# Sum of squares of y taken along the rows of a transposed copy, a prologue that projects the first half of x before the second is normed, and the row order 7, 3, 6, 2, 5, 1, 4, 0

## Chip, core and metric

One core of one Trainium2 chip. The metric is the device time of one execution in microseconds (us). The three runs of the kernel before took 556.85, 557.12 and 557.29 us; their median is 557.12.

## What is computed

`xn` is the layer norm of x (1024 rows of 256). Sixteen heads of width 128 attend causally over it, and a small 256 x 256 product of `xn` is added; the sum with x is the output.

```python
q = (x @ Wq).reshape(B, T, H, D)
k = (x @ Wk).reshape(B, T, H, D)
v = (x @ Wv).reshape(B, T, H, D)
q = rmsnorm(q, q_rms_w)
k = rmsnorm(k, k_rms_w)
scores = jnp.einsum('bthd,bshd->bhts', q, k) * scale + bias[None]
scores = jnp.where(causal[None, None], scores, -jnp.inf)
attn = jax.nn.softmax(scores, axis=-1)
y = jnp.einsum('bhts,bshd->bhtd', attn, v)
y = rmsnorm(y, subln_w)
y = y.transpose(0, 2, 1, 3).reshape(B, T, H * D)
return y @ Wproj
```

`rmsnorm` divides a row by the root of the mean of its squares. This is the place of the change: for each head and each row of y the kernel needs the sum of 128 squares.

## The kernel before

The program is written out by hand, engine by engine, with semaphores. x is cut into 8 row tiles of 128 rows. Every fp32 product is made of three fp32r matmuls, high by high, high by low and low by high (`product`, L469 to L473), so each operand is stored as a high part (rounded by ScalarE) and a low part (the rest, by VectorE or GpSimd).

Each engine runs the same two-level loop: 16 heads, and in a head 8 steps s. `ORDER` (L33) says which row tile i a step works on; row tile i has i+1 blocks of 128 columns, because of the causal mask. A step on TensorE holds: the scores of the next step's row (`score`, L531), one or two of the eight projections of the next head (`project`, L504: six matmuls of 384 columns, q, k and v together), a part of the attention product (`attend`, L555), and at the end the transposes of this step's probabilities (`transpose_probs`, L544). The eight rows form two groups of four, `GROUPS`: the first four of `ORDER` and the last four. `attend` multiplies a group by v, in two halves, into the one bank `yT_ps`; y comes out transposed, 128 columns of D on the partitions and 4 x 128 rows along the free side. The second group of a head is attended to in steps 0 and 1 of the next head.

y is normed late. ScalarE squares `yT_ps` (`y_out`, L755) into `y_sq`; since D lies on the partitions there, the sum over D is a matmul: `sum_squares` (L576) multiplies four tiles of `y_sq` by a column of ones, which the trace shows as eight matmuls with one output column each. VectorE adds EPS times the squared row sum (`y_mean`, L907), GpSimd takes the power -0.5 (`norm_y`, L422), and VectorE scales the output product by it when it adds that to `acc` (`add_out`, L916). `sum_squares` of group 0 stands at step 0 of the next head, in the bank `qkv_ps`, that of group 1 at step 4, in `yT_ps`.

The engines' other work in a head: ScalarE copies each projection out (`copy_qkv`, L714), squares q and k, takes the exponentials (`exps`, L739) and the high parts. VectorE adds bias and takes the row maximum (`mask`, L874), makes the low parts (`probs_lo`, `qk_lo`, `y_lo`) and the sums of the q and k squares (`mean_squares`, L854). GpSimd splits weights and v and norms q and k (`norm_qk`, L382), whose result `transpose_qk` (L521) waits for. `score` of a next head's first row waits for the last `qk_lo`.

Prologue: x comes in two transfers. VectorE takes the moments of half 0, then of half 1, then norms half 0 (`normed`, L943), and later half 1. TensorE runs 24 warming matmuls, transposes all of x (`transpose_x`, L605) and only then projects the head 0. The fp8 weights are decoded by eight VectorE operations (L982 to L989) before the first `mean_squares`.

Of the kernel before, what the change touches and what calls it, by code (L numbers as in the profile page):

```python
# [13 lines left out]
def build_block(nc, x, wq, wk, wv, wproj, q_w, k_w, sub_w, ffn_w, ffn_ws, ffn_xs, out):  # L14
# [18 lines left out]
    ORDER = [7, 0, 6, 1, 5, 2, 4, 3]  # L33
# [16 lines left out]

    def misc_done(h, job):
# [5 lines left out]
        base = NPAIR + len(MISC_FIRST) + (h - 1) * len(MISC)  # L57
        if isinstance(h, int) and h == H - 1:
            return base + MISC_LAST.index(job) + 1
        if isinstance(h, int) and h == H:  # L60
            return base - len(MISC) + len(MISC_LAST) + MISC_TAIL.index(job) + 1
        return base + MISC.index(job) + 1
# [7 lines left out]
    with ctx:  # L70
# [11 lines left out]
        ones = sb("ones", [P, 1])  # L82
# [31 lines left out]
        y_sq = sb("y_sq", [P, 2, 4 * P])  # L114
# [23 lines left out]
        x_loaded = [sem(f"x_loaded{n}") for n in range(2)]  # L138
# [52 lines left out]
        ss_ready = sem("ss_ready")  # L191
# [34 lines left out]
        WARM_UP = 24  # L226

# [21 lines left out]
        def squares_of(h, k):  # L249

            if isinstance(h, int) and h == 0 and k % 2:
                return y_sq[:, 0, :].rearrange("p (t n) -> p t n", t=2)
# [32 lines left out]
        def _(sp):  # L285
            for n in range(2):
                half = slice(n * NT // 2, (n + 1) * NT // 2)
                sp.dma_start(acc[:, half, :], x_v[:, half, :]).then_inc(x_loaded[n], 16)
# [32 lines left out]
        def _(pool):  # L321
# [20 lines left out]
            pool.memset(ones[:, :], 1.0)  # L342
            for h in range(H):
                pool.memset(slopes[:, h:h + 1], float(np.float32(2.0 ** (-0.5 * (h + 1)))))

            for n in range(2):
# [4 lines left out]

            link(pool.iota(dist[:, :], pattern=[[-1, T]], base=T - P, channel_multiplier=1,
                           allow_small_or_imprecise_dtypes=True))
            pool.affine_select(out=dist[:, :], in_=dist[:, :], compare_op=ALU.is_ge, fill=BIG, base=T - P,
                               pattern=[[-1, T]], channel_multiplier=1).then_inc(const_ready, 1)
# [66 lines left out]
            def norm_y(h, g, now):  # L422

                pool.wait_ge(misc_read, misc_done(now, f"ss{g}"))
# [38 lines left out]
            norm_y(H - 1, 0, H)  # L463
            norm_y(H - 1, 1, H)
# [3 lines left out]
        def _(pe):  # L468
# [6 lines left out]
            def bank_free(h, job):  # L475
# [17 lines left out]
                if same:  # L493
# [10 lines left out]
            def project(h, par, k):  # L504
# [8 lines left out]
                if k == 1 and not (isinstance(h, int) and h <= 1):  # L513
                    pe.wait_ge(misc_read, misc_done(h - 1, "ss0"))
# [40 lines left out]
            def attend(h, par, g, half):  # L555
# [4 lines left out]
                if half == 0:  # L560
# [4 lines left out]
                    if g == 0 and not (isinstance(h, int) and h == 0):  # L565
                        pe.wait_ge(misc_read, misc_done(h, "ss1"))
# [32 lines left out]
            for _ in range(WARM_UP):  # L599
                pe.matmul(score_big[:, 0:4 * P], ident_b[:, :], ident_b[:, :].unsqueeze(1).broadcast_to([P, 4, P]),  # L600
                          start=True, stop=True)
# [11 lines left out]
            for n in range(2 * KT):  # L613
                transpose_x(n)
# [484 lines left out]
```

## Time and profile before

| | before |
|---|---|
| median of three runs | 557.12 us |
| the profiled execution | 556.8 us, of which the span of the trace 554.7 |
| granted TensorE clock, mean of the span | 0.991 |
| TensorE matmul busy | 531.1 us (96%) |
| TensorE weight loads busy | 492.5 us (89%) |
| VectorE busy | 414.6 us (75%) |
| ScalarE busy | 376.0 us (68%) |
| GpSimd busy | 333.8 us (60%) |
| the chain that ended last | TensorE 77%, GpSimd 9%, issue 4%, VectorE 3%, ScalarE 3% |

The chain of waits is followed back from the last instruction. Matmuls overlap one another: a matmul's duration in a row is from its start to its end in the array, while what it costs the stream is the distance to the start of the next one.

### The profile page before, as it was taken

To read this page: it belongs to the slowest core of one execution; us is meant where nothing else is said; L and a number is where in the kernel's file an instruction comes from. 1 tells how busy PE (TensorE), PEld (TensorE's weight loads), DVE (VectorE), ACT (ScalarE), POOL (GpSimd) and SP (SyncE) were. 2 spreads that over 40 slices of the span, in tenths; PEclk is the share of its full clock that TensorE was granted. 3 is DMA by queue.
4 is the path that set the end of the run, shared out by engine and by line. 5 is a ranking of instruction groups with operands and counts; after the bars stand their busy time and mean duration, and the time that the engine had idled before them with its cause. 6 is when DMAs were issued, how large, how long until landed. Compare 5 with 4: busy or idle time off the path is not lost.

```text
span 554.7 us, 12030 instructions
## 1 busy us (share of the span) xinstructions
PE 531.1 (96%) x3548; PEld 492.5 (89%) x3548; DVE 414.6 (75%) x999; ACT 376.0 (68%) x855; POOL 333.8 (60%) x431
## 2 busy tenths in 40 slices
PE   5768999999999999999999999999999999999996
PEld 2758899999989999998999999899999989999885
DVE  5867778686777868777786867778687786878765
ACT  2367778685776868577686857768685776858561
POOL 3386487683748658483776837486584847748121
PEclk9799999999999999999999999999999999999999
DMA  5100101001010100101010010101001000000002
GB/s 159 54 2 1 39 1 38 3 1 40 2 39 0 38 0 0 38 0 38 0 38 0 0 38 0 38 0 32 6 0 38 0 9 0 9 1 1 1 1 77
DMA packets 18582, 10.83 MB, mean 20 GB/s; under 512 B 2176, under 2 KB 18560, under 8 KB 18560
## 3 DMA queue, kind: packets, MB, share of 16 engines
q1 hardware_dynamic: 17568, 10.49, 6.3%
q8 instruction: 11, 0.18, 0.1%
q10 hardware_dynamic: 992, 0.07, 0.1%
q14 instruction: 11, 0.09, 0.1%
HBM read 9.51 MB, written 1.05 MB: 19 GB/s over the span
## 4 chain that ended last, share of the span: by engine, by line
PE 77%; POOL 9%; issue 4%; DVE 3%; ACT 3%; DMA 1%; POOLq 1%; DVEq 0%; SPq 0%
PE pT_ps L551 9%; PE qkv_ps L471 9%; PE qkv_ps L473 8%; PE qkv_ps L472 8%; PE yT_ps L473 6%; PE yT_ps L472 6%; PE yT_ps L471 6%; PE score_big L471 4%; PE score_big L473 4%; PE score_big L472 4%; PE misc L527 3%; POOL qk_n L220 3%; POOL qk_r L385 3%; PE qkv_ps L580 2%; PE yT_ps L580 2%
## 5 line engine op out<-in xcount | busy, mean ns | idle before, releaser
L723 ACT ACTIVATE stage<-qkv_ps 128x384 f32<-128x384 f32 x119 | 58.6, 493 | 91.1 <-PE qkv_ps L473 90.6
L897 DVE TENSOR_TENSOR pT_lo<-pT_ps,pT_hi 128x384 fp32r<-128x384 f32 (+1 forms) x192 | 100.9, 554 | 25.2 <-ACT pT_hi L751 23.3
L751 ACT ACTIVATE pT_hi<-pT_ps 128x384 fp32r<-128x384 f32 (+1 forms) x192 | 86.3, 484 | 46.7 <-PE pT_ps L551 42.9
L425 POOL TENSOR_TENSOR y_r<-y_ms,minus_half 128x4 f32<-128x4 f32 x32 | 32.8, 1026 | 136.1 <-DVE y_ms L913 136.1
L743 ACT ACTIVATE probs<-probs,neg_max 128x1024 f32<-128x1024 f32 (+7 forms) x128 | 98.4, 770 | 8.2 <-DVE neg_max L888 7.6
L551 PE MATMUL pT_ps<-ident,probs 128*128 128x128 f32 x576 | 85.7, 276 | 4.0 <-ACT probs L743 3.3
L471 PE MATMUL qkv_ps<-w_hi,xT_hi 128*128 128x384 f32 x242 | 87.3, 361 | 0.6 <-ACT stage L723 0.6
L473 PE MATMUL qkv_ps<-w_hi,xT_lo 128*128 128x384 f32 x242 | 81.9, 338 | 0.0
L472 PE MATMUL qkv_ps<-w_lo,xT_hi 128*128 128x384 f32 x242 | 81.8, 338 | 0.0
L385 POOL TENSOR_TENSOR qk_r<-qk_ms,minus_half 128x4 f32<-128x4 f32 x64 | 65.0, 1015 | 26.8 <-DVE qk_ms L862 26.0
L551 PEld LDWEIGHTS pT_ps<-ident,probs 128*128 128x128 f32 x576 | 66.8, 143 | 10.9 <-DVE pT_lo L897 4.2
L471 PE MATMUL yT_ps<-pT_hi,v_hi 128*128 128x256 f32 (+1 forms) x224 | 71.7, 320 | 0.4 <-DVE pT_lo L897 0.4
L473 PE MATMUL yT_ps<-pT_hi,v_lo 128*128 128x256 f32 (+1 forms) x224 | 71.9, 321 | 0.0
L472 PE MATMUL yT_ps<-pT_lo,v_hi 128*128 128x256 f32 (+1 forms) x224 | 71.7, 320 | 0.0
L859 DVE TENSOR_REDUCE qk_ms<-squares 128x4 f32<-128x512 f32 x62 | 42.5, 685 | 37.2 <-ACT squares L730 36.9
L888 DVE CUSTOM_DVE_ANT_0 probs<-score_big,bias 128x1024 f32<-128x1024 f32 (+1 forms) x64 | 65.0, 1016 | 1.9 <-PE score_big L473 1.9
L220 POOL TENSOR_TENSOR qk_n<-stage,qk_r 128x512 f32<-128x512 f32 x60 | 62.4, 1040 | 5.7 <-POOL qk_r L385 1.9
L402 POOL TENSOR_TENSOR v_lo<-stage,v_hi 128x256 fp32r<-128x256 f32 x62 | 46.6, 752 | 9.0
L471 PE MATMUL score_big<-kT_hi,qT_hi 128*128 128x512 f32 (+2 forms) x128 | 50.3, 393 | 1.8 <-DVE kT_lo L871 1.7
L471 PEld LDWEIGHTS qkv_ps<-w_hi,xT_hi 128*128 128x128 f32 x242 | 46.2, 191 | 2.1 <-ACT stage L723 0.9
L472 PEld LDWEIGHTS qkv_ps<-w_lo,xT_hi 128*128 128x128 f32 x242 | 45.9, 190 | 0.0
L473 PEld LDWEIGHTS qkv_ps<-w_hi,xT_lo 128*128 128x128 f32 x242 | 45.7, 189 | 0.0
(182 smaller groups left out, 1308.6 us busy)
## 6 DMA issues: line engine op xcount, KB each, us to landing
w_raw<-in_wq SPq DMA_DIRECT2D x16, 128.0 KB, 2.2
w_raw<-in_wk SPq DMA_DIRECT2D x16, 128.0 KB, 2.3
w_raw<-in_wv SPq DMA_DIRECT2D x16, 128.0 KB, 2.3
wp_raw<-in_wproj SPq DMA_DIRECT2D x16, 128.0 KB, 2.0
acc<-in_x SPq DMA_DIRECT2D x2, 512.0 KB, 5.5
out<-acc SPq DMA_DIRECT2D x8, 128.0 KB, 1.8
w<-in_ffn_w ACTq DMA_DIRECT2D x1, 64.0 KB, 6.2
q_col<-in_q_w ACTq DMA_DIRECT2D x1, 0.5 KB, 3.0
```

The lines of the kernel that those rows point to most:

```text
L220: eng.tensor_tensor(qk_n[:, k % 2], stage_of(h, k)[:, :, 0:2 * D].rearrange("p t (a d) -> p t a d", d=D), qk_r[:, k % 2, :].rearrange("p ( ...
L385: pool.tensor_tensor(qk_r[:, k % 2, :], qk_ms[:, k % 2, :], minus_half[:, 0:4], ALU.pow).then_inc(qk_r_ready, 1)
L402: pool.tensor_tensor(v_lo[:, par, 2 * k:2 * k + 2, :], v, v_hi[:, par, 2 * k:2 * k + 2, :].bitcast(f32), ALU.subtract).then_inc(v_split, 1)
L471: pe.matmul(dst, a_hi, b_hi, start=start, stop=False)
L472: pe.matmul(dst, a_hi, b_lo, start=False, stop=False)
L473: return pe.matmul(dst, a_lo, b_hi, start=False, stop=stop)
L551: last = pe.transpose(ps[:, (j - a) * P:(j - a + 1) * P], probs[:, s % 2, j * P:(j + 1) * P], ident[:, :])
L723: act.activation(stage_of(h, k // 2)[:, k % 2, :], qkv_bank(h, k)[:, 0:3 * D], ACT.Copy).then_inc(qkv_read, 1)
L743: act.activation(probs[:, s % 2, 0:(i + 1) * P], probs[:, s % 2, 0:(i + 1) * P], ACT.Exp, bias=neg_max[:, par, s:s + 1], scale=-1.0, accum ...
L751: act.activation(pT_hi[g][:, a:b, r * P:(r + 1) * P], pT_ps[(CHUNK0[s] + k) % 2][:, 0:(b - a) * P].rearrange("p (j t) -> p j t", t=P), ACT ...
L888: dve.tensor_tensor_reduce(out=probs[:, s % 2, 0:w], in0=ps[:, at:at + w], in1=bias[:, par, (NT - 1 - i) * P:(NT - 1 - i) * P + w], scale= ...
L897: dve.tensor_tensor(pT_lo[g][:, a:b, r * P:(r + 1) * P], pT_ps[(CHUNK0[s] + k) % 2][:, 0:(b - a) * P].rearrange("p (j t) -> p j t", t=P), ...
```

## The change

1. `sum_squares` goes. `y_out` now copies `yT_ps` unsquared into `y_raw`; TensorE turns it by four fp32 transposes (`turn_y`) into the bank where the sums stood; ScalarE squares the turned bank into one buffer `y_sq` (`square_y`), and VectorE reduces that along the free side (in `y_mean`). `square_y` of group 0 stands on ScalarE at step 1 behind `exps`, that of group 1 at step 4. `y_mean` moves from steps 0 and 4 to 1 and 5. On GpSimd `norm_y` of group 0 moves behind the weight split, that of group 1 behind the last `norm_qk`. Banks are released by `square_y` instead of `y_mean`.
2. `ORDER` is now 7, 3, 6, 2, 5, 1, 4, 0, so the groups are {7, 6, 3, 2} and {5, 4, 1, 0} instead of {7, 6, 1, 0} and {5, 4, 3, 2}.
3. In the prologue x comes in four transfers; VectorE norms half 0 before it takes the moments of half 1; TensorE transposes half 0, runs 10 more warming matmuls, projects row tiles 0 and 1 and only then transposes half 1; GpSimd makes the distance table ahead of the norms and begins its first weight split only when all of x is normed.
4. The decoding of the fp8 weights moves into the steps of head 0, one or two operations in each.

```diff
-    ORDER = [7, 0, 6, 1, 5, 2, 4, 3]
+    ORDER = [7, 3, 6, 2, 5, 1, 4, 0]
...
             pool.wait_ge(w_split, 1)
+            pool.wait_ge(xn_ready, NT)
             split_w(1, 1)
...
-                if not first:
-                    norm_y(h - 1, 0, h)
                 if tile is not None:
                     round_x(tile)
                 if not (isinstance(h, int) and h + 2 >= H):
                     split_w(h + 2, par)
+                if not first:
+                    norm_y(h - 1, 0)
...
-                if not first:
-                    norm_y(h - 1, 1, h)
                 if not last:
                     norm_qk(h + 1, NPAIR - 1)
+                if not first:
+                    norm_y(h - 1, 1)
...
-            def sum_squares(h, g, now):
+            def turn_y(h, g, now):
                 bank_free(now, f"ss{g}")
-                pe.wait_ge(y_squared, 2 * h + g + 1)
+                pe.wait_ge(y_copied, 2 * h + g + 1)
                 for r in range(4):
-                    last = pe.matmul(job_ps(h + 1, f"ss{g}")[:, r:r + 1], y_sq[:, g, r * P:(r + 1) * P], ones[:, 0:1],
-                                     start=True, stop=True)
-                last.then_inc(ss_ready, 1)
+                    last = pe.transpose(job_ps(h + 1, f"ss{g}")[:, r * P:(r + 1) * P], y_raw[:, g, r * P:(r + 1) * P],
+                                        ident[:, :])
+                last.then_inc(y_turned, 1)
...
-            for n in range(2 * KT):
-                transpose_x(n)
+            transpose_x(0)
+            transpose_x(1)
+            warm(KEEP_WARM)
             for k in range(NT):
...
                 project(0, 0, k)
+                if k == 1:
+                    transpose_x(2)
+                    transpose_x(3)
...
+            def square_y(h, g):
+                act.wait_ge(y_turned, 2 * h + g + 1)
+                past(act, y_summed, 2 * h + g)
+                act.activation(y_sq[:, :], job_ps(h + 1, f"ss{g}"), ACT.Square).then_inc(y_squared, 1)
...
+                dve.wait_ge(y_squared, 2 * h + g + 1)
+                dve.tensor_reduce(y_ms[:, g, :], y_sq[:, :].rearrange("p (r d) -> p r d", d=D),
+                                  AX.X, ALU.add).then_inc(y_summed, 1)
```

What stands in the engines' rows at three places. First TensorE at the start of the program (`ident_b` is the warming matmul, `bias` holds the normed x, `xT` its transposed parts). Before:

```order
L600 MATMUL score_big<-ident_b 128x512 x24
L609 MATMUL pT_ps<-ident,bias 128x128 x8
L609 MATMUL misc<-ident,bias 128x128 x4
L609 MATMUL score_small<-ident,bias 128x128 x4
L471 MATMUL qkv_ps<-w_hi,xT_hi 128x384
```

With the change:

```order
L614 MATMUL score_big<-ident_b 128x512 x24
L625 MATMUL pT_ps<-ident,bias 128x128 x8
L614 MATMUL score_big<-ident_b 128x512 x10
L479 MATMUL qkv_ps<-w_hi,xT_hi 128x384
...
L481 MATMUL yT_ps<-w_hi,xT_lo 128x384
L625 MATMUL misc<-ident,bias 128x128 x4
L625 MATMUL score_small<-ident,bias 128x128 x4
```

The eight transposes of half 1 moved behind the first two projections, and ten warming matmuls stand before these.

Second ScalarE in head 1, from the copy of the first projection through the exponentials of steps 0 and 1 to the first high parts (the row widths show the order). Before:

```order
L723 ACTIVATE stage<-qkv_ps 128x384
L743 ACTIVATE probs,row_sum<-probs,neg_max 128x1024
L743 ACTIVATE probs,row_sum<-probs,neg_max 128x128
L751 ACTIVATE pT_hi<-pT_ps 128x4x128 x2
L723 ACTIVATE stage<-qkv_ps 128x384
L730 ACTIVATE squares<-stage 128x512
```

With the change:

```order
L743 ACTIVATE stage<-qkv_ps 128x384
L763 ACTIVATE probs,row_sum<-probs,neg_max 128x1024
L763 ACTIVATE probs,row_sum<-probs,neg_max 128x512
L783 ACTIVATE y_sq<-qkv_ps 128x512
L771 ACTIVATE pT_hi<-pT_ps 128x4x128 x2
L743 ACTIVATE stage<-qkv_ps 128x384
L750 ACTIVATE squares<-stage 128x512
```

The exponentials of step 1 grew from 128 to 512 columns, and the square of the turned y stands between them and the high parts.

Third VectorE in steps 5 and 6 of head 0, up to the last low parts of q and k. Before:

```order
L888 ISA probs,neg_max<-score_big,bias 128x640
L888 ISA neg_max 128x1
L897 TENSOR_TENSOR pT_lo<-pT_ps,pT_hi 128x3x128
L869 SCALAR_TENSOR_TENSOR qT_lo<-qkv_ps,q_col,qT_hi 128x256
L871 TENSOR_TENSOR kT_lo<-qkv_ps,kT_hi 128x256
L888 ISA probs,neg_max<-score_small,bias 128x512
L888 ISA neg_max 128x1
L869 SCALAR_TENSOR_TENSOR qT_lo<-misc,q_col,qT_hi 128x256
```

With the change:

```order
L925 ISA probs,neg_max<-score_big,bias 128x640
L925 ISA neg_max 128x1
L1042 TENSOR_SCALAR wb<-y_raw 128x512
L934 TENSOR_TENSOR pT_lo<-pT_ps,pT_hi 128x2x128
L906 SCALAR_TENSOR_TENSOR qT_lo<-qkv_ps,q_col,qT_hi 128x256
L908 TENSOR_TENSOR kT_lo<-qkv_ps,kT_hi 128x256
L925 ISA probs,neg_max<-score_small,bias 128x128
L925 ISA neg_max 128x1
L1044 TENSOR_TENSOR y_raw<-y_raw,wb 128x512
L1045 SCALAR_TENSOR_TENSOR wb<-y_raw 128x512
L906 SCALAR_TENSOR_TENSOR qT_lo<-misc,q_col,qT_hi 128x256
```

Three operations of the fp8 decoding came in, two of them right ahead of the last low parts of q, and the mask of step 7 shrank from 512 to 128 columns.

## Rows read from the trace of the kernel before

**Rows 1.** Busy time by stretch: us long, then each engine's busy us, granted clock

```profile
13.00:19.40 6.40, 1.49 (x7) 1.49 (x8) 6.12 (x7) 0.34 (x1) 4.47 (x4) 0.50 0.36 102
64.07:518.64 454.57, 453.43 (x3073) 425.00 (x3070) 346.61 (x835) 325.44 (x744) 290.48 (x357) 1.00 0.05 14
```

**Rows 2.** Timeline of TensorE in head 5: start us, duration us, engine, instruction

```profile
198.52 1.07 PE L551 MATMUL pT_ps<-ident,probs 128*128 128x128 f32 x8
199.34 0.47 PE L471 MATMUL score_big<-kT_hi,qT_hi 128*128 128x512 f32 x1
199.66 0.39 PE L472 MATMUL score_big<-kT_lo,qT_hi 128*128 128x512 f32 x1
199.88 0.40 PE L473 MATMUL score_big<-kT_hi,qT_lo 128*128 128x512 f32 x1
...
213.14 0.95 PE L580 MATMUL yT_ps<-ones,y_sq 128*128 128x1 f32 x8
213.95 0.42 PE L471 MATMUL qkv_ps<-w_hi,xT_hi 128*128 128x384 f32 x1
214.21 0.34 PE L472 MATMUL qkv_ps<-w_lo,xT_hi 128*128 128x384 f32 x1
```

**Rows 3.** Who waited for whom: total us, times, longest us

```profile
PEld misc L527 <- POOL qk_n L220: 6.1, 12, 0.5
```

**Rows 4.** Groups by line: count, busy us, mean ns of one, idle before

```profile
L859 DVE TENSOR_REDUCE qk_ms<-squares 128x4 f32<-128x512 f32 x62 | 42.5, 685 | 37.2 <-ACT squares L730 36.9
L757 ACT ACTIVATE y_sq<-yT_ps 128x512 f32<-128x512 f32 x32 | 19.1, 597 | 4.3 <-PE yT_ps L473 4.3
```

**Rows 5.** Timelines of three engines, end of head 5 and start of head 6

```profile
213.34 0.49 ACT L723 ACTIVATE stage<-qkv_ps 128x384 f32<-128x384 f32 x1 [0.16 <-PE qkv_ps L473]
...
221.51 0.68 DVE L888 CUSTOM_DVE_ANT_0 probs<-score_small,bias 128x512 f32<-128x512 f32 x1
...
222.63 0.41 DVE L871 TENSOR_TENSOR kT_lo<-misc,kT_hi 128x256 fp32r<-128x256 f32 x1
...
223.78 0.48 PE L471 MATMUL score_big<-kT_hi,qT_hi 128*128 128x512 f32 x1
...
226.54 0.22 PE L471 MATMUL score_small<-kT_hi,qT_hi 128*128 128x128 f32 x1
...
226.82 0.39 PE L471 MATMUL qkv_ps<-w_hi,xT_hi 128*128 128x384 f32 x1
...
228.40 0.28 DVE L888 CUSTOM_DVE_ANT_0 probs<-score_small,bias 128x128 f32<-128x128 f32 x1
...
228.67 1.14 ACT L743 ACTIVATE probs<-probs,neg_max 128x1024 f32<-128x1024 f32 x1
...
230.84 0.42 PE L551 MATMUL pT_ps<-ident,probs 128*128 128x128 f32 x2
```

**Rows 6.** Timelines of the front, up to the first scores

```profile
7.28 1.02 POOL L349 TENSOR_TENSOR rstd<-rstd,minus_half 128x4 f32<-128x4 f32 x1 [4.84 <-DVE rstd L941]
...
9.25 1.38 DVE L946 TENSOR_SCALAR bias<-acc,mean_var,rstd 128x256 f32<-128x256 f32 x4
...
12.89 4.96 DVE L946 TENSOR_SCALAR bias<-acc,mean_var,rstd 128x256 f32<-128x256 f32 x4 [0.91 <-POOL rstd L349]
...
19.53 0.67 PE L471 MATMUL qkv_ps<-w_hi,xT_hi 128*128 128x384 f32 x1
...
28.97 0.34 PE L473 MATMUL yT_ps<-w_hi,xT_lo 128*128 128x384 f32 x1
...
36.64 0.50 PE L471 MATMUL score_big<-kT_hi,qT_hi 128*128 128x512 f32 x1 [1.69 <-DVE kT_lo L871]
```

**Rows 7.** Timelines at the end of head 0

```profile
61.50 0.42 DVE L871 TENSOR_TENSOR kT_lo<-misc,kT_hi 128x256 fp32r<-128x256 f32 x1
...
61.97 0.50 PE L471 MATMUL score_big<-kT_hi,qT_hi 128*128 128x512 f32 x1
```

**Rows 8.** Groups by line, the last operation of the fp8 decoding

```profile
L989 DVE SCALAR_TENSOR_TENSOR wb<-y_sq 128x512 bf16<-128x512 f32 x1 | 0.7, 691 | 0.0
```

More of the change, by code:

```diff
@@ L49, in build_block, with freed @@
     MISC_TAIL = ["ss0", "proj0a", "ss1", "proj0b", "proj1a", "proj1b"]
+    def freed(jobs):
+        return [m for m in jobs if not m.startswith("ss")]
     def misc_done(h, job):
@@ L136, in build_block @@
         misc = pb("misc", [P, 512])
-        x_loaded = [sem(f"x_loaded{n}") for n in range(2)]
+        x_loaded = [sem(f"x_loaded{n}") for n in range(4)]
         small_loaded = sem("small_loaded")
@@ L285, in _ @@
         def _(sp):
-            for n in range(2):
-                half = slice(n * NT // 2, (n + 1) * NT // 2)
-                sp.dma_start(acc[:, half, :], x_v[:, half, :]).then_inc(x_loaded[n], 16)
+            for n in range(4):
+                quarter = slice(n * NT // 4, (n + 1) * NT // 4)
+                sp.dma_start(acc[:, quarter, :], x_v[:, quarter, :]).then_inc(x_loaded[n], 16)
             def load_w(h, par):
@@ L492, in bank_free @@
                 same = [m for m in jobs[:jobs.index(job)] if bank_of(h, m) == bank and (m != "ss0" or tail)]
-                if same:
+                if is_last(h) and job == "proj1a":
+                    pe.wait_ge(y_squared, 2 * h - 1)
+                if same and same[-1].startswith("ss"):
+                    pe.wait_ge(y_squared, 2 * h - 1 + int(same[-1][2]))
+                elif same:
                     pe.wait_ge(misc_read, misc_done(h, same[-1]))
@@ L598, in _, with warm @@
             pe.wait_ge(const_ready, 2)
-            for _ in range(WARM_UP):
-                pe.matmul(score_big[:, 0:4 * P], ident_b[:, :], ident_b[:, :].unsqueeze(1).broadcast_to([P, 4, P]),
-                          start=True, stop=True)
+            def warm(count):
+                for _ in range(count):
+                    pe.matmul(score_big[:, 0:4 * P], ident_b[:, :], ident_b[:, :].unsqueeze(1).broadcast_to([P, 4, P]),
+                              start=True, stop=True)
+            warm(WARM_UP)
             def transpose_x(n):
@@ L777, in _, with round_xT @@
             act.activation(w_hi[:, 0], w_raw[:, 0], ACT.Copy).then_inc(w_hi_done, 1)
-            for n in range(2 * KT):
+            def round_xT(n):
                 half, kt = n // KT, n % KT
@@ L804, in head @@
                         exps(h, par, s)
+                    if s == 1 and not first:
+                        square_y(h - 1, 0)
                     if s > 0:
@@ L818, in head @@
                         exps(h, par, s)
+                    if s == 4 and not first:
+                        square_y(h - 1, 1)
                     if s == 5 and not last:
@@ L836, in head @@
                     if s == 7:
+                        if first:
+                            act.wait_ge(wb_ready, 1)
                         y_out(h, 0)
@@ L947, in normed, with split_xT @@
                                       ALU.subtract, ALU.mult).then_inc(xn_ready, 1)
-            moments(0)
-            variances(0)
-            moments(1)
-            normed(0)
-            variances(1)
-            dve.wait_ge(w_hi_done, 1)
-            dve.tensor_tensor(w_lo[:, 0], w_raw[:, 0], w_hi[:, 0].bitcast(f32), ALU.subtract).then_inc(w_split, 1)
-            normed(1)
-            dve.wait_ge(small_loaded, 80)
-            dve.scalar_tensor_tensor(q_col[:, 2:3], q_col[:, 0:1], -SCALE, q_col[:, 1:2],
-                                     ALU.mult, ALU.mult).then_inc(wq_col_ready, 1)
-            for n in range(2 * KT):
+            def split_xT(n):
                 half, kt = n // KT, n % KT
@@ L967, in _ @@
                                   ALU.subtract).then_inc(xT_read, 1)
+            moments(0)
+            variances(0)
+            normed(0)
+            moments(1)
+            variances(1)
+            split_xT(0)
+            dve.wait_ge(w_hi_done, 1)
+            dve.tensor_tensor(w_lo[:, 0], w_raw[:, 0], w_hi[:, 0].bitcast(f32), ALU.subtract).then_inc(w_split, 1)
+            split_xT(1)
+            normed(1)
+            dve.wait_ge(small_loaded, 80)
+            dve.scalar_tensor_tensor(q_col[:, 2:3], q_col[:, 0:1], -SCALE, q_col[:, 1:2],
+                                     ALU.mult, ALU.mult).then_inc(wq_col_ready, 1)
+            split_xT(2)
+            split_xT(3)
             def step_of_x(t):
@@ L1035, in head @@
                         mask(h + 1, 1 - par, 0)
+                    if first:
+                        decode_w8(s)
                     if first and s == 4:
@@ L1043, in head @@
                             add_out(h - 2, 1, 1)
+                    if s == 1 and not first:
                         y_mean(h - 1, 1 - par, 0)
@@ L1050, in head @@
                         mean_squares(h + 1, 0)
-                    if s == 4 and not first:
+                    if s == 5 and not first:
                         y_mean(h - 1, 1 - par, 1)
```

98 lines of the change are left out of this document (58 added, 40 removed).

## Prediction

> **What bounds the kernel now.** I read the busy time by stretch first. From the start of head 1 to the start of head 15 (64.07 to 518.64) TensorE is busy 453.43 of 454.57 us at a granted clock of 1.00 [rows 1]. That is 14 heads of 32.47 us each. VectorE has 346.61 and ScalarE 325.44 us of work in the same stretch, so both have room on average, and the question is only where each must be on time. Since matmuls overlap, busy time alone does not show that TensorE's stream is dense; the distances between starts do. In the timeline of head 5 a 512-column matmul follows the last after 0.22 to 0.23 us [rows 2], and a 384-column one by its share after 0.17. By such distances the stream of a head adds up to about 32.0 us; some 0.4 us of a head is left for waits. The one that the list of waits names most is TensorE's weight load for the q and k transposes behind GpSimd's norm, 6.1 us in 12 times [rows 3].
>
> The front is different. From 13.00 to 19.40 the granted clock is 0.50, the lower of its two levels, 1.2 instead of 2.4 GHz [rows 1]: TensorE did 1.49 us of matmuls in these 6.40, waiting for a norm of half 1 of x that took VectorE 4.96 us where half 0 took 1.38 [rows 6].
>
> **Part 1, the sum of squares on TensorE.** Before, a group of eight one-column matmuls runs from 213.14 to the next start at 213.95, 0.81 us, and the 384-column matmul behind it is followed only after 0.26 instead of 0.17 us, so the group costs 0.90 us [rows 2]. Eight fp32 transposes run from 198.52 to 199.34, 0.82 us, and the matmul after them is followed after 0.32 instead of 0.22, so eight cost 0.92 and one about 0.114 [rows 2]. Four cost 0.46. A group thus gets cheaper by 0.45 us, a head by 0.90. In 14 heads that is 12.6 us on the engine that sets the pace.
>
> A lone transpose is longer than its share of a row: eight that last 1.07 us in all, with 0.11 from start to start, leave about 0.27 for one [rows 2]. The Trainium skill, "TensorE: Matmul & The Clock Gate", Part 4, gives about 275 ns for a transpose in a kernel. Read as a cost in the stream that would make four of them 1.1 us and the change a loss here; the trace agrees with 0.27 as a duration and contradicts it as a distance.
>
> **What it puts on the other engines.** The first ScalarE pass over `yT_ps` stays as long as it was (a copy for a square). New are a square of 128x512 out of PSUM, 0.60 us by the old one, and a VectorE reduce of 128x512, 0.69 us by that of the q and k squares [rows 4]. I take 0.5 us of ScalarE's and 0.8 to 1.0 us of VectorE's time for each group. Twice a head this brings VectorE from 24.8 to about 26.6 us and ScalarE from 23.2 to 24.2 of a 32 us period: neither becomes the bound on average. The places where one is late:
>
> (a) Step 0. The exponentials of row 7 run 228.67 to 229.81, and TensorE comes to their transposes at 230.84, a slack of one us [rows 5]. Now the scores ahead of the first projection are those of row 3, 3 x 0.23 = 0.70 us instead of 0.28 (226.54 to 226.82), which moves ScalarE's copy and the exponentials 0.4 later. TensorE in between does less: the first half of the second group is three matmuls of 512 and three of 384 columns, 1.22 us, where nine of 512 took 2.10, and the turn of y saves 0.45. It arrives at 230.84 + 0.42 - 0.88 - 0.45 = 229.93, while the exponentials are through at 229.81 + 0.42 + 0.1 = 230.3. A new wait of 0.3 to 0.4 us.
>
> (b) Step 4. The last projection waits for the copy of the one before, which runs 213.34 to 213.83, and starts at 213.95 [rows 5, 2]. With 0.45 less ahead of it, TensorE comes at 213.50: a new wait of 0.3 us.
>
> (c) Steps 5 and 6. The reduce of group 1 stands ahead of the last low parts of k, which now end at 223.04, while the next head's first scores start at 223.78 [rows 5]. The reduce and its two small neighbours add 1.0 us, and the mask of step 7 has 128 columns instead of 512, 0.28 instead of 0.68 us [rows 5]. TensorE itself comes about 0.3 later, with four blocks of attention more (12 x 0.058 = 0.7 us) and three score matmuls of 512 columns made 128 (0.4 less). Of the 0.74 us of slack some 0.4 is left, so no wait, but this is the tightest place.
>
> (d) GpSimd: with the norm of y behind that of q and k, the wait of 0.5 us [rows 3] goes; it was overlapped in part, and I count 0.25 to 0.3. Moving the other norm of y behind the weight split costs nothing, since the output addition that needs it comes a step later.
>
> Sum for a head: -0.90 + 0.35 + 0.3 - 0.3 - 0.15 (the other small waits of before, which a later TensorE would meet and an earlier one partly doesn't) gives -0.70. **Fourteen heads: -9.8 us.** The bounds: -1.3 a head if every wait goes, old ones too, and 0 if the waits eat it all.
>
> **Part 2, the row order.** Numbers and widths of all matmuls in a head stay the same: both groups together have 36 blocks before and after, and widths 4 x 512, 2 x 384, 6 x 256, 2 x 128. It moves work from the second group to the first (18 and 18 blocks to 22 and 14) and is priced in (a) to (c).
>
> **Part 3, the front.** GpSimd's first power ends at 8.30 and half 0 was normed only at 9.25, behind the moments of half 1; half 1 ended at 17.85 [rows 6]. Now: half 0 normed from 8.35 or earlier (x lands in quarters) for 1.4 us, transposes done at 10.7; VectorE's moments of half 1, two low parts of xT and the low weights come to 4.2 us (an estimate by columns from a pass of 0.69 us over 512 [rows 4]: 1.4, 1.4 and 1.0, and 0.4 for the small ones) and end near 13.9; the first projection starts at about 13.6 to 14.0 instead of 19.53. Half 1 is normed beside the first projections in 1.4 us, since GpSimd waits for it. From the first start to the last project matmul, 19.53 to 28.97, the eight projections took 9.4 us, some at the low clock [rows 6]; now they take 8 x 1.05 plus eight transposes, 9.3. So the projections end 6 us earlier, and from there to the first scores at 36.64 the same chain of square, sum, power and norm follows, without the decoding ahead of it: **-6.3 us.**
>
> **Part 4, the decoding in head 0.** The last low parts of k end at 61.92 and the scores start right then, at 61.97: no slack [rows 7]. Two decoding operations of 0.69 us [rows 8] and a cheaper one now come ahead of them, 1.7 us by my count, less the 0.4 us of the smaller mask and the 0.3 that TensorE itself is later by. **+0.9 us.** The other five lie in VectorE's idle time of head 0.
>
> **The end.** Head 15 has no projections, so it is a chain; it gains its share of 0.9 and pays the new square and reduce, -0.2. After it TensorE has 0.45 us less to turn and four blocks less to attend (12 x 0.058 = 0.7); the chain into the last power gets a square and a reduce and loses four matmuls, +0.85. **-0.5 us together.**
>
> Sum: -6.3 + 0.9 - 9.8 - 0.5 = -15.7. Against the profiled execution's 556.8 that is 541.1; the median of the runs is 0.3 above it, so **541.4 us**.
>
> **Rivals.** (A) No new waits: the slacks are larger than I read, and even the old ones go. -1.3 x 14 = -18.2, with the front and the end 533.2 us. For it: both engines are under 80% busy. Against: (a) and (b) come out of single rows. 12%.
> (B) ScalarE and VectorE eat most of the gain in the heads: a wait behind (c) as well, which leaves 0 to -0.3 a head, 547 to 551 us. For it: slack in (c) is less than half a us, and GpSimd's accesses stretch some VectorE operations, as in the front. 14%.
> (C) The clock falls in the front all the same, as it did before [rows 1]; TensorE's gap there is a us or two now, but if two projections run at half speed, that adds 2 us: 543.4. It lies inside the forecast's range. 6%.
> (D) **Slower**: square and reduce lie on the path in both groups, since VectorE gets behind. The place is the reduce ahead of the last low parts of k; the price 2 x (0.60 + 0.69) - 0.90 = +1.7 us a head, +23.8 in all, less 5.9 elsewhere: 575. It decides from +0.42 a head on (5.9 over 14). Against: VectorE idles a fifth of each head. 5%.
> (E) **Slower** too: the transposes of y follow each other at their duration, 0.27 us, instead of at 0.11: 4 x 0.27 + 0.09 = 1.17 a group, +0.54 a head instead of -0.90, +0.74 with the waits: +10.4 - 5.9 = 4.5, 561.6 us. Against: the same kind of instruction [rows 2]. 2%. The Trainium skill's clock gate page would be read rightly as a cost then.
> (F) The change doesn't do what it says, as that the front is held by its transfers (x in quarters costs two more issues ahead of the weights) and heads as in (B): no difference, 556 to 558. 2%.
>
> **How the numbers follow.** The forecast has 59%; its own range is 536 to 546. The range 534.5 to 550 leaves out half of (A), a third of (B) and (D) to (F), some 2 in 10. Faster is all but (D), (E), (F): 0.91. Within 0.2% (1.1 us, about what a measurement of this kernel can tell from no change) 0.02. Slower 0.07.
>
> **What would show it.** Groups of four transposes from `y_raw` at 0.45 us and heads of 31.6 to 31.9 us: part 1 right. A wait of TensorE for the exponentials at step 0 and for the copy at step 4 of each head, 0.3 us each: (a) and (b). First projection near 14 us with clock 1.00, both halves of x normed in 1.4 us, first scores near 30.4: part 3. A wait of about a us for `kT_lo` at the end of head 0: part 4. A wait for `kT_lo` in every head would mean (B) or (D).

## The result and the profile after

The changed kernel takes 549.31 us (median of four runs, 549.21 to 549.56), the kernel before beside it 556.99 us. The ratio is 0.9864, with a 95% interval of 0.9847 to 0.9881: faster by 7.7 us, where 15.7 was forecast. The profiled execution has a span of 547.2 us where before it was 554.7, so 7.5 us are to be found in the trace.

| stretch | before | after | moved by | forecast |
|---|---|---|---|---|
| start to the first scores | 36.64 | 31.08 | -5.56 | -6.3 |
| head 0, from there to the start of head 1 | 27.43 | 29.68 | +2.25 | +0.9 |
| head 1 to the start of head 15 | 454.57 | 450.34 | -4.23 | -9.8 |
| head 15 and the end | 36.05 | 36.14 | +0.1 | -0.5 |

So the miss lies in the heads above all. The windows of the changed kernel, in the columns of [rows 1]:

```profile
14.20:19.40 5.20, 5.20 (x33) 5.16 (x34) 3.03 (x8) 2.92 (x6) 2.67 (x2) 1.00 0.36 102
60.76:511.10 450.34, 444.82 (x2961) 413.12 (x2958) 347.38 (x862) 335.26 (x772) 290.49 (x357) 1.00 0.05 14
```

In [rows 1] TensorE was busy 453.43 of 454.57 us. Now it is busy 444.82 of 450.34. The matmul time did fall, by 8.6 us in 14 heads, but 5.5 us of the stretch are idle where 1.1 were. The list of waits of the changed kernel has two near its top that were small in the kernel before (total, times, longest; PEld is TensorE's weight load, the part of a matmul that waits first):

```profile
PE pT_ps L564 <- ACT probs L763: 6.7, 17, 1.0
PEld qkv_ps L479 <- ACT stage L743: 6.2, 15, 0.9
```

Both are waits for ScalarE, 15 times or more, about once in each head. Before, the first came 4 times with 3.3 us in all and the second once. The timeline of TensorE shows where they are. The first turn of y in head 5, at step 0, before (the eight one-column matmuls, which the transposes of row 7 at 198.52 follow [rows 2]):

```profile
197.71 0.95 PE L580 MATMUL qkv_ps<-ones,y_sq 128*128 128x1 f32 x8
```

and after, there and at step 4:

```profile
192.52 0.60 PE L593 MATMUL qkv_ps<-ident,y_raw 128*128 128x128 f32 x4
193.40 1.09 PE L564 MATMUL pT_ps<-ident,probs 128*128 128x128 f32 x8 [0.28 <-ACT probs L763]
...
208.55 0.34 PE L481 MATMUL qkv_ps<-w_hi,xT_lo 128*128 128x384 f32 x1
208.74 0.60 PE L593 MATMUL yT_ps<-ident,y_raw 128*128 128x128 f32 x4
209.48 0.44 PE L479 MATMUL qkv_ps<-w_hi,xT_hi 128*128 128x384 f32 x1
```

Read the starts. At step 0 the sum on TensorE took 197.71 to 198.52, 0.81 us; the four transposes with what follows them take 192.52 to 193.40, 0.88 us. Four transposes with more transposes behind them are 0.44 (q and k, 206.53 to 206.97), so TensorE stands still for 0.44 us. At step 4 the group took 213.14 to 213.95, 0.81 us [rows 2], and now 208.74 to 209.48, 0.74. Four transposes with a matmul behind them are 0.36 (shown under e9_old_rows_between), so 0.38 is waiting. The two places together cost 1.62 us a head before and 1.62 after. What they wait for stands in ScalarE's timeline:

```profile
192.04 1.14 ACT L763 ACTIVATE probs<-probs,neg_max 128x1024 f32<-128x1024 f32 x1
193.08 0.19 ACT L763 ACTIVATION_READ_ACCUMULATOR probs<-probs,neg_max 128x1 f32 x1
...
208.52 0.39 ACT L757 ACTIVATE kT_hi<-misc 128x256 fp32r<-128x256 f32 x1
208.93 0.49 ACT L743 ACTIVATE stage<-qkv_ps 128x384 f32<-128x384 f32 x1
```

The exponentials of row 7 are through at 193.27, and the transposes start at 193.40. The copy of the projection before runs from 208.93 to 209.42, and the last projection starts at 209.48. What a head did gain, 0.30 us, stands at step 6. Before, TensorE's last score matmul and the transposes of q and k behind it:

```profile
219.88 0.40 PE L473 MATMUL score_small<-kT_hi,qT_lo 128*128 128x512 f32 x1
220.35 0.33 PE L527 MATMUL misc<-ident,qk_n 128*128 128x128 f32 x1
```

and after:

```profile
215.53 0.28 PE L481 MATMUL score_small<-kT_hi,qT_lo 128*128 128x128 f32 x1
215.65 0.41 PE L540 MATMUL misc<-ident,qk_n 128*128 128x128 f32 x2
```

A 512-column matmul is followed after 0.23 us, so of 0.47 before 0.24 were a wait; after, 0.12 is the plain distance of a 128-column one. This wait is the one for GpSimd's norm [rows 3]; the transposes behind it now also follow each other without delay, 0.03 to 0.05 us more.

Two theories follow. Theory W: the cheaper turns are spent waiting for ScalarE, and the heads' gain is GpSimd's norm. Its rival, theory G: the cheaper turns are the gain, and something else eats a part.

### The profile page after: what moved, and what is told of

The parts are those of the page before. It is cut to its first block, busy times and chain, and to the rows that moved or that the text cites. A ratio compares the mean times of both kernels' runs of the same rounds, so it can differ in the third digit from the quotient of the medians.

```text
span 547.2 us, 11888 instructions
## 1 busy us (share of the span) xinstructions
PE 521.8 (95%) x3430; PEld 477.3 (87%) x3430; DVE 416.0 (76%) x1031; ACT 388.0 (71%) x887; POOL 334.3 (61%) x430
## 4 chain that ended last, share of the span: by engine, by line
PE 81%; ACT 7%; DVE 5%; issue 3%; DMA 1%; POOL 0%; ACTq 0%; POOLq 0%; DVEq 0%; SPq 0%
PE pT_ps L564 12%; PE qkv_ps L479 9%; PE qkv_ps L481 8%; PE qkv_ps L480 8%; PE yT_ps L481 6%; PE yT_ps L480 6%; PE yT_ps L479 6%; PE score_big L479 4%; PE score_big L481 4%; PE score_big L480 4%; ACT probs L763 4%; PE misc L540 3%; ACT stage L743 2%; PE score_small L480 2%; PE score_small L481 2%
## 5 line engine op out<-in xcount | busy, mean ns | idle before, releaser
L934 DVE TENSOR_TENSOR pT_lo<-pT_ps,pT_hi 128x512 fp32r<-128x512 f32 (+2 forms) x192 | 100.9, 554 | 41.7 <-ACT pT_hi L771 39.7
L771 ACT ACTIVATE pT_hi<-pT_ps 128x512 fp32r<-128x512 f32 (+2 forms) x192 | 86.1, 483 | 42.6 <-PE pT_ps L564 42.5
L564 PEld LDWEIGHTS pT_ps<-ident,probs 128*128 128x128 f32 x576 | 65.4, 140 | 18.8 <-issue 8.3
```

The source lines that it names most:

```text
L564: last = pe.transpose(ps[:, (j - a) * P:(j - a + 1) * P], probs[:, s % 2, j * P:(j + 1) * P], ident[:, :])
L771: act.activation(pT_hi[g][:, a:b, r * P:(r + 1) * P], pT_ps[(CHUNK0[s] + k) % 2][:, 0:(b - a) * P].rearrange("p (j t) -> p j t", t=P), ACT ...
L934: dve.tensor_tensor(pT_lo[g][:, a:b, r * P:(r + 1) * P], pT_ps[(CHUNK0[s] + k) % 2][:, 0:(b - a) * P].rearrange("p (j t) -> p j t", t=P), ...
```

## The experiments

The heads of each run are measured in its trace, from the start of head 1 to that of head 15, over 14. Every one of the 14 heads has the waits that are read from one of them below, so this is sharper than the times. Ratios are to the kernel before, run beside each, with their 95% intervals.

| kernel | time, us | ratio | us a head |
|---|---|---|---|
| before | 556.99 | | 32.47 |
| after | 549.31 | 0.9864 (0.9847 to 0.9881) | 32.17 |
| e1_norm_only | 552.35 | 0.9921 (0.9903 to 0.9940) | 32.15 |
| e2_old_rows | 545.24 | 0.9793 (0.9767 to 0.9818) | 31.86 |
| e3_score_between | 547.76 | 0.9840 (0.9822 to 0.9858) | 32.03 |
| e4_cut3 | 544.21 | 0.9785 (0.9769 to 0.9802) | 31.85 |
| e6_new_rows_only | 556.03 | 0.9998 (0.9988 to 1.0007) | 32.49 |
| e7_decode_late | 548.32 | 0.9857 (0.9840 to 0.9873) | 32.19 |
| e8_turn_twice | 550.16 | 0.9885 (0.9867 to 0.9904) | 32.21 |
| e9_old_rows_between | 541.95 | 0.9749 (0.9729 to 0.9769) | 31.56 |
| e10_decode_late | 540.37 | 0.9710 (0.9694 to 0.9727) | 31.57 |
| e12_decode_early | 540.61 | 0.9715 (0.9699 to 0.9731) | 31.59 |
| e13_new_rows_early | 541.28 | 0.9725 (0.9709 to 0.9742) | 31.69 |
| e14_norm_back | 627.63, one run | | 37.8 |

### The norm alone

On the kernel before:

```diff
-                if not first:
-                    norm_y(h - 1, 1, h)
                 if not last:
                     norm_qk(h + 1, NPAIR - 1)
+                if not first:
+                    norm_y(h - 1, 1, h)
```

> The kernel before with one thing of the change: GpSimd takes the last norm of q and k ahead of the norm of y. Theory W (the cheaper turns of y are spent waiting for ScalarE, and what a head gained is this norm's wait): TensorE's wait of 0.24 us ahead of the last q and k transposes goes, a head falls from 32.43 to 32.2 us, 14 heads give 3.4 us, the time is 553.4 us. Theory G (the cheaper turns are the gain, and something else eats part of it): the wait was mostly covered, 0 to 1 us, 556 us or more.

A head takes 32.15 us, 0.32 less than before, as short as one of the changed kernel. Swapping two calls of GpSimd gives all that the whole change gave in the heads. At step 6 the wait is gone:

```profile
218.94 0.39 PE L473 MATMUL score_small<-kT_hi,qT_lo 128*128 128x512 f32 x1
219.17 0.60 PE L527 MATMUL misc<-ident,qk_n 128*128 128x128 f32 x4
```

### Each turn twice

On the changed kernel:

```diff
-                for r in range(4):
+                for r in [r for r in range(4) for _ in range(2)]:
```

> The changed kernel with each transpose of y done twice, eight where there were four, 0.46 us more in each of two places of a head. Theory W: the extra ones lie in the waits of 0.44 and 0.38 us, a head grows by 0.1 us, the time by 1.5 to 2.5 us (551 to 552). Theory G: each costs its full time, 0.92 us a head, 13.7 us in all, 563.

The time grows by 1.2 us by the ratios, a head by 0.04 us: theory W. The timeline of TensorE, at both places:

```profile
192.61 1.03 PE L593 MATMUL qkv_ps<-ident,y_raw 128*128 128x128 f32 x8
193.49 1.09 PE L564 MATMUL pT_ps<-ident,probs 128*128 128x128 f32 x8
...
208.80 1.03 PE L593 MATMUL yT_ps<-ident,y_raw 128*128 128x128 f32 x8
209.59 0.42 PE L479 MATMUL qkv_ps<-w_hi,xT_hi 128*128 128x384 f32 x1
```

Eight transposes and no wait take 192.61 to 193.49, the same 0.88 us as four and a wait. At step 4 eight take 0.79 us, where four and a wait took 0.74. The waits had been as long as the added work, to within 0.05 us.

### The row order

e2_old_rows is the changed kernel with `ORDER = [7, 0, 6, 1, 5, 2, 4, 3]`; e6_new_rows_only is the kernel before with the new order.

> The changed kernel with the old row order 7, 0, 6, 1, 5, 2, 4, 3. Theory W: nine attention matmuls of 512 columns are back ahead of the first turn, TensorE comes later than the exponentials of row 7, and the wait of 0.44 us at step 0 goes: a head falls from 32.17 to about 31.75 us, 543.5 us in all; if VectorE's 512-column mask of step 7 now makes TensorE wait for the low part of k (up to 0.3 us), 547. A theory by which the row order costs nothing: 549.

> The kernel before with the new row order alone. Theory W: the group of one-column matmuls is still 0.8 us long, so TensorE reaches the transposes of row 7 at 230.38 by the rows of before and the exponentials are through at 230.33: no wait, and the time stays at 556.4, 555.5 to 557.5 us. Theory R (the row order itself costs the 0.31 us a head that its undoing gave on the changed kernel): 560.7 us.

With the old order a head falls from 32.17 to 31.86. TensorE at step 0, with nine attention matmuls of 512 columns ahead of it:

```profile
192.59 0.60 PE L593 MATMUL qkv_ps<-ident,y_raw 128*128 128x128 f32 x4
193.03 1.04 PE L564 MATMUL pT_ps<-ident,probs 128*128 128x128 f32 x8
```

0.44 us and no wait; the wait at step 4 stays, 0.39 us (207.68 to 208.43, less 0.36). A small wait for the low part of k did come in. At the end of the head, VectorE and then TensorE:

```profile
217.63 0.41 DVE L908 TENSOR_TENSOR kT_lo<-misc,kT_hi 128x256 fp32r<-128x256 f32 x1
```

```profile
217.59 0.71 PE L564 MATMUL pT_ps<-ident,probs 128*128 128x128 f32 x5
218.17 0.49 PE L479 MATMUL score_big<-kT_hi,qT_hi 128*128 128x512 f32 x1
```

The low part ends at 218.04, and the scores start 0.58 us after the five transposes, where they started 0.47 after them in e1_norm_only. In 12 of 14 heads the scores start 0.13 us behind the low part; in the changed kernel, whose mask of step 7 has 128 columns instead of 512, 0.33 us lie between the two. On the kernel before, the same new order costs nothing (32.49 to 32.47): there the group of one-column matmuls was long enough to cover the exponentials. So the row order takes away slack, and only the shorter turn makes that slack count; neither alone makes the wait at step 0. With the old order the sum of squares does pay: e2_old_rows against e1_norm_only, both with the norm moved, is 31.86 to 32.15, 0.29 us a head. That is the 0.82 us that the turns save, less the 0.39 at step 4 and some 0.13 for the low part of k. With the new order it pays nothing: in head 5 the changed kernel and e6_new_rows_only run alike to within 0.02 us up to step 6, where the norm's wait of 0.25 us makes the difference.

### Other work ahead of the wait

e4_cut3, on the changed kernel, three more matmuls before the first turn:

```diff
-                cut = next(j for j in range(nj + 1) if 2 * sum(weight[:j]) >= sum(weight))
+                cut = 3 if g == 1 else next(j for j in range(nj + 1) if 2 * sum(weight[:j]) >= sum(weight))
```

> The changed kernel with the second group's attention cut after three blocks of v instead of two, so that three matmuls of 256 columns (0.35 us) run ahead of the turn of y at step 0 instead of behind it. Theory W: the wait of 0.46 us for the exponentials of row 7 falls to 0.11, a head loses 0.35 us, 549.3 - 4.9 = 544.4 us. Rival (the exponentials move along with TensorE, or another wait takes over): within 1 us of 549.3.

0.32 us a head, where 0.35 was expected, and 4.4 us by the ratios (5.1 by the medians). From the start of the turn to that of the next transposes it is now 191.30 to 191.81, 0.51 us, so 0.07 are left of the wait:

```profile
191.30 0.60 PE L593 MATMUL qkv_ps<-ident,y_raw 128*128 128x128 f32 x4
191.81 0.33 PE L564 MATMUL pT_ps<-ident,probs 128*128 128x128 f32 x1
```

e3_score_between moves the scores of step 4 behind project 6:

```diff
-                    if s < NT - 1:
+                    if s < NT - 1 and (s != 4 or first or last):
                         score(h, par, s + 1)
...
                             project(h + 1, 1 - par, 2 * s - 2)
+                        if s == 4 and not first and not last:
+                            score(h, par, s + 1)
```

> The changed kernel with the scores of step 5's row put between project 6 and the turn of y in step 4, so that ScalarE's copy has 0.44 us more of other work ahead of project 7. Theory W: the wait of 0.38 us there goes and nothing comes for it: a head falls by 0.35 us, 549.3 - 4.9 = 544.4 us. Rival: project 6 now waits for the copy of project 5, or the mask comes late, and the time stays within 1 us of 549.3.

A miss: 0.14 us a head instead of 0.35. ScalarE's timeline shows why (`kT_hi` is the last high part, `stage` the copy):

```profile
207.77 0.39 ACT L759 ACTIVATE kT_hi<-misc 128x256 fp32r<-128x256 f32 x1
208.03 0.50 ACT L745 ACTIVATE stage<-qkv_ps 128x384 f32<-128x384 f32 x1
```

The copy no longer waits for TensorE; it starts as soon as ScalarE is through with the high parts of q and k that stand ahead of it. The other work covered the wait until ScalarE's own queue became the limit, and 0.19 us of it stayed (the turn takes 208.04 to 208.59, less 0.36). The rival has a share too: project 6 now comes just as the copy of project 5 ends, which costs 0.06 us. With the old row order the same move puts 384 instead of 256 columns there:

> The changed kernel with the old row order and with the scores between project 6 and the turn of y. With the old order these scores are 384 columns wide, 0.61 us, more than the wait of 0.33 us that e2_old_rows still has there. Theory W: no wait at either turn, a head falls from 31.86 to 31.53 us, 545.2 - 4.6 = 540.6 us. Rival, as e3_score_between showed: ScalarE's own queue ahead of the copy leaves 0.13 us or more of the wait, 542.5 us or more.

31.56 us a head, 0.30 less than e2_old_rows, where 0.33 was forecast. In head 5 the turn takes 205.38 to 205.74, with no wait behind it:

```profile
205.38 0.60 PE L593 MATMUL yT_ps<-ident,y_raw 128*128 128x128 f32 x4
205.74 0.42 PE L479 MATMUL qkv_ps<-w_hi,xT_hi 128*128 128x384 f32 x1
```

About 0.16 us is lost ahead of project 6, which now comes before the copy of project 5 is done. The time, 541.95, is the median of runs from 541.02 to 542.89, and lies 1.3 above the forecast.

### Decoding in head 0

At the end of head 0 of the changed kernel VectorE runs these, and TensorE (the fence of one row) waits:

```profile
56.20 0.85 DVE L1044 TENSOR_TENSOR y_raw<-y_raw,wb 128x512 f32<-128x512 f32 x1
57.09 1.10 DVE L1045 SCALAR_TENSOR_TENSOR wb<-y_raw 128x512 bf16<-128x512 f32 x1
58.11 0.47 DVE L906 SCALAR_TENSOR_TENSOR qT_lo<-misc,q_col,qT_hi 128x256 fp32r<-128x256 f32 x1
58.50 0.41 DVE L908 TENSOR_TENSOR kT_lo<-misc,kT_hi 128x256 fp32r<-128x256 f32 x1
```

```profile
58.97 0.50 PE L479 MATMUL score_big<-kT_hi,qT_hi 128*128 128x512 f32 x1 [1.56 <-DVE kT_lo L908]
```

e7_decode_late puts the two operations behind `qk_lo(h + 1, 1 - par, 3)`:

> The changed kernel with the last two decoding operations of head 0 behind the last low parts of k instead of ahead of them. If they are what TensorE waited 1.56 us for there: the wait is gone, the transposes of the weights come a little later, and the time falls by 1.2 to 1.5 us, to 548.0. If head 1's start is held by something else: 549.3.

Head 1 starts at 59.54 instead of 60.76, and head 0 is 1.04 us shorter in the trace. The wait of 1.56 us is gone, and one of 0.60 us for the low parts of the probabilities, which now stand behind the decoding, has come. The time is 0.4 (by the ratios) to 1.0 us less, too little for the intervals to part from none, so that the gain rests on the trace. On top of e9_old_rows_between, once with the two operations late as in e7 and once with all of the decoding early (the edit of the latter):

```diff
                     if first:
-                        decode_w8(s)
+                        for part in {0: (0, 1, 2), 1: (3,), 2: (4,), 3: (5, 6)}.get(s, ()):
+                            decode_w8(part)
```

> e9_old_rows_between with the last two decoding operations behind the last low parts of k, as in e7_decode_late. There they gave 1.0 us; here TensorE waits 2.1 us for these low parts at the end of head 0, 1.8 of it for the two operations. 541.95 - 1.3 = 540.6 us.

> e9_old_rows_between with the decoding in the first four steps of head 0 (three operations in step 0, one each in steps 1 and 2, three in step 3), where VectorE idles 1.2 and 0.9 us. If what counts is only that nothing of it lies in steps 4 to 7: the wait of 2.1 us at the end of head 0 goes and nothing comes for it, 541.95 - 2.0 = 540.0 us. If VectorE's lateness from step 3 is carried to the end of the head, or the operations get longer beside GpSimd's: 541 or more.

540.37 and 540.61: no difference that can be told. Head 0, 29.36 us in e9_old_rows_between, is 28.18 and 28.48. Early decoding takes the wait at the end of head 0 away and puts one of 0.88 us in the middle (48.09 to 49.14): the transposes of the second pair of q and k want the bank `misc`, whose last reader on VectorE is through only at 49.09. e10_decode_late is the fastest kernel of this study, 2.9% under the kernel before, and its 1.6% under the changed kernel come from the old row order, the moved scores and the moved decoding. The new row order gets nearly as far once its waits are covered:

> The changed kernel with its new row order, the attention cut of e4_cut3, the scores of e3_score_between and the early decoding of e12. Theory W, adding the waits: e4 gave 5.1, e3 1.5 to 1.9, decoding 1.0 to 1.5: 549.3 - 8 = 541.3 us. If the waits don't add (the one at step 4 grows when the one at step 0 goes): 543 or more.

541.28 us, and 31.69 us a head: 32.17 less the 0.32 of e4_cut3 and the 0.14 of e3_score_between is 31.71. The gains at step 0 and 4 add up as measured one by one.

### The norm of y back

On the changed kernel, `norm_y(h - 1, 1)` ahead of the last `norm_qk`, as it was.

> The changed kernel with GpSimd's norm of y back ahead of the last norm of q and k, as it was before. The mean of y is now ready only at 216.4 us of the changed kernel's head 5 (a square on ScalarE and a reduce on VectorE came ahead of it), so q and k would be normed at 219.6 instead of 215.1 while TensorE wants them at 215.65: a wait of 4.0 us a head, 15 times, 549.3 + 60 = 609 us. If the order matters only by the 0.24 us that it cost before: 553 us.

627.63 us, in one run, where 609 was expected. Once the sum of squares goes by way of ScalarE and VectorE, its order on GpSimd is no longer a matter of 0.24 us: the move is part of the change, not an extra. The wait itself is as forecast (TensorE):

```profile
238.94 0.27 PE L481 MATMUL score_small<-kT_hi,qT_lo 128*128 128x128 f32 x1
243.06 0.66 PE L540 MATMUL misc<-ident,qk_n 128*128 128x128 f32 x4 [3.84 <-POOL qk_n L227]
```

but a head grew by 5.6 us, not 4.0. The windows of this run show the rest (after the length: TensorE's matmuls and weight loads, VectorE, ScalarE, GpSimd, then the clock and the DMA columns):

```profile
238.90:243.06 4.16, 0.32 (x4) 0.18 (x2) 2.12 (x8) 1.83 (x5) 3.07 (x4) 1.00 0.00 0
243.06:243.80 0.74, 0.74 (x6) 0.73 (x7) 0.00 (x0) 0.04 (x1) 0.74 (x1) 0.93 0.00 0
243.80:247.00 3.20, 3.20 (x16) 3.20 (x15) 0.81 (x2) 1.08 (x4) 2.65 (x6) 0.50 0.13 36
247.00:250.60 3.60, 3.60 (x25) 3.08 (x25) 2.21 (x5) 2.02 (x5) 0.17 (x1) 0.98 0.40 113
```

After the wait the granted clock falls to 0.50, the 1.2 GHz level, for some 3.2 us, in which TensorE does what it would do in 1.6.

## Why the prediction was wrong

**Part 1, the price of a group: nearly right.** Before, the group took 0.81 us. I had counted 0.90 for both groups, adding the late follower of the matmul behind. At step 0 transposes stand behind the group, and they pay that hand-over themselves: 0.81 against 0.44, a saving of 0.37 and not 0.45. At step 4 it is 0.81 against 0.36, with the same late follower in both, 0.45 as forecast. That makes 0.82 a head instead of 0.90.

**(a) and (b): right in place and cause, too small.** The wait at step 0 is 0.44 us where I said 0.3 to 0.4, that at step 4 0.38 where I said 0.3. Together 0.82 instead of 0.65, so that of the saving of 0.82 nothing is left. This is the first of the two terms that failed: 0.25 us a head was to remain of the cheaper turns, and the waits for ScalarE took all of it.

**(d), right**: a wait of 0.24 us, and 0.32 a head when e1_norm_only takes it away alone. **The "-0.15" for other small waits: wrong**, the second term that failed. It had no row. The late starts of 0.08 to 0.12 us in a head before are each the second matmul behind transposes, and they are there after, too; with the norm's wait gone, e1_norm_only still needs 32.15 us a head. So the sum for a head is -0.82 + 0.82 - 0.30 + 0 = -0.30, which is what was measured. In 14 heads the step "gives -0.70" is off by 5.6 us, of the 8.2 in all.

**(c), right**: no wait for the low part of k in any head from 1 on, with 0.33 us of slack left where I said 0.4. It wasn't the tightest place. With the old row order it is a wait of some 0.13 us (e2_old_rows).

**The load on the other engines: ScalarE's right, VectorE's too large.** ScalarE is busy 23.9 us of a head where I said 24.2, VectorE 24.8, as before, where I said 26.6. The two reduces of 0.68 us came in as priced, but small operations of 128x4 got shorter, two kinds of them from 0.46 to 0.20 and from 0.27 to 0.17 us in the mean, and more of the operations overlap their neighbours.

**Part 2, the row order: priced in the right places, but never against its own absence.** (a) has TensorE arrive 0.88 us earlier for it and the exponentials 0.4 later, and e2_old_rows shows that the wait at step 0 is the row order's. What I didn't ask is what the change would give without it. It costs nothing on the kernel before (e6_new_rows_only) and 0.31 us a head with the shorter turn.

**Part 3, the front: -5.56 for -6.3.** The mechanism holds (TensorE's and VectorE's rows, changed kernel):

```profile
14.20 0.44 PE L479 MATMUL qkv_ps<-w_hi,xT_hi 128*128 128x384 f32 x1 [0.73 <-DVE xT_lo L994]
...
23.35 0.34 PE L481 MATMUL yT_ps<-w_hi,xT_lo 128*128 128x384 f32 x1
...
31.08 0.50 PE L479 MATMUL score_big<-kT_hi,qT_hi 128*128 128x512 f32 x1 [1.69 <-DVE kT_lo L908]
```

```profile
7.46 0.17 DVE L982 TENSOR_SCALAR rstd<-mean_var 128x4 f32<-128x4 f32 x1
8.77 1.39 DVE L987 TENSOR_SCALAR bias<-acc,mean_var,rstd 128x256 f32<-128x256 f32 x4 [1.14 <-POOL rstd L361]
...
14.06 1.37 DVE L987 TENSOR_SCALAR bias<-acc,mean_var,rstd 128x256 f32<-128x256 f32 x4
```

The projections run at clock 1.00 (the window above) and half 1 is normed in 1.37 us where it took 4.96 [rows 6]. But half 0 is normed from 8.77, not 8.35: VectorE waited 0.99 us for the second quarter of x, and the input of the first power was begun at 7.46 instead of 7.03. The projections end 5.62 us earlier, not 6. And the chain from there to the first scores, which I had a little shorter without the decoding ahead of it, is 7.73 us where it was 7.67. No run here undoes one part of the front, so how the 5.56 us divide among the order of the norms, the transfers and the warming matmuls is not shown.

**Part 4, head 0: +2.25 for +0.9.** The wait is the one named, 1.56 us with the two operations stretched from 0.69 to 0.85 and 1.10. The row order has no part in it: e6_new_rows_only has a head 0 of 27.43 us, as the kernel before, and undoing the order on the changed kernel makes head 0 longer (30.07 us in e2_old_rows). Its 0.7 us more of attention there are made up by shorter waits for exponentials (1.02 and 0.52 us instead of 1.42 and 0.96), and it has a wait of 0.22 for the low part of k. Against that kernel, 1.34 of the 2.25 is the longer wait for the low part of k. A second wait, which I hadn't named, is at step 6, 0.48 us by the starts:

```profile
54.32 0.63 PE L540 MATMUL misc<-ident,qk_n 128*128 128x128 f32 x4 [0.33 <-POOL qk_n L227]
```

GpSimd's norm is late there because VectorE begins the sum that it needs only at 51.09, behind the operations at 48.96 and 50.43 that the last section shows. The rest, about 0.4 us, is in smaller pieces: transposes that take 1.20 us at 40.43 where seven took 0.98, and late starts of a tenth or less.

**The end: +0.1 for -0.5.** From the start of TensorE's last matmul to the end of the span it is 5.4 us instead of 4.5, the +0.85 of the forecast. In head 15, which has no projections, TensorE waits for exponentials at three steps (0.32, 0.48 and 0.99 us; before at two, 0.33 and 0.59), and of some 1.5 us less work it keeps 0.8. That 0.8 is the row order's: e6_new_rows_only, with the old sum of squares, has it too (35.26 us for head 15 and the end, where the kernel before has 36.05).

**The rivals.** (B) comes nearest, 0 to -0.3 a head: ScalarE ate the gain, but by (a) and (b), not by a wait behind (c). (A), (D), (E) and (F) are out. For (E): where no wait stands behind them, four transposes of y take 0.44 us ahead of more transposes (e2_old_rows) and 0.36 ahead of a matmul (e9_old_rows_between), 0.09 to 0.11 each. For (C): the clock was 1.00 from the first projection to the last of the front. The 533.2 of (A) should by its own terms be 533.0, which changes nothing.

## What to carry to other kernels

On the engine that sets the pace, a shorter group of instructions is worth the smaller of two numbers: what it saves, and the slack of whatever the next instruction behind it waits for; read that slack before the saving is added, and count no remainder that has no row. Where the slack is the smaller, move other ready work between the producer and its user; that works until the helping engine's own queue is the limit. To learn whether an edit paid, put the saved work back in: if the time stands still, the saving had gone into a wait. And where a change has several parts, price each against its own absence: here the row order cost nothing alone and took 0.31 us a head together with the shorter turn.

## What the runs showed of the hardware

**The clock after a wait.** Waits of 2.30 us (56.67 to 58.97, five transposes in it) and 1.68 us in head 0 and the front of the changed kernel left the granted clock at 1.00. In e14_norm_back one of 4.1 us was followed by 3.2 us at 0.50, which cost 1.6 us more; the 3.0 us behind the same wait in seven other heads have a mean clock of 0.50 to 0.64. The Trainium skill, "TensorE: Matmul & The Clock Gate", Part 1, has the lower clock as the default that activity releases; the trace of e14_norm_back agrees, with 1.00 before the wait and 0.50 after it.

**VectorE beside GpSimd.** In head 0 of the changed kernel, like operations took very unlike times (VectorE, then GpSimd). The second row's operation took 0.43 us in the kernel before:

```profile
44.70 0.42 DVE L1038 TENSOR_SCALAR y_raw<-y_raw 128x512 int32<-128x512 int32 x1
48.96 1.05 DVE L1040 TENSOR_SCALAR y_raw<-y_raw 128x512 f32<-128x512 f32 x1
50.43 0.73 DVE L1098 TENSOR_TENSOR ffn_s<-ffn_s 128x1 f32<-128x1 f32 x1
```

```profile
48.69 1.04 POOL L227 TENSOR_TENSOR qk_n<-stage,qk_r 128x512 f32<-128x512 f32 x1
50.41 0.74 POOL L409 TENSOR_TENSOR v_lo<-stage,v_hi 128x256 fp32r<-128x256 f32 x1
```

GpSimd's first operation ends at 49.73, and the one of VectorE that began inside it lasts to 50.01; the second ends at 51.15, and the product of one column at 51.16, though the reciprocal of one column just ahead of it took 0.17 us. The Trainium skill, "SBUF — State Buffer", section "Who interferes with whom", says that VectorE operations with two inputs in SBUF, or in a mode that uses two ports, share a pair of ports with GpSimd, and that in such a mode whoever issues first holds the pair for its whole instruction. The rows agree: in both cases GpSimd's operation had started first, by 0.27 and 0.02 us. Rival (B) had that stretch in mind. It is probably also what made the two operations of part 4 0.57 us longer together, since GpSimd was at work on SBUF tiles beside them; no run here takes GpSimd's work away to show it.
